# Batch 0's first score maxima from fp32 products instead of packed bf16 rows, with the splitting on GpSimd and values and batch 1's queries moved into the main loop

## The reference, cut to what matters

```python
x = x + tanh(g_xattn[0]) * attention(layernorm(x), ctx, ctx, Wq, Wk, Wv, Wo)
#   qh = einsum('bnd,hde->bhne', q, Wq);  kh, vh likewise from ctx with Wk, Wv
#   att = softmax(qh @ kh.T * 0.125);     out = concat_h(att @ vh) @ Wo.T
x = x + tanh(g_ffn[0]) * ffn(layernorm(x), router_w, w1, b1, w2, b2)
#   softmax over 8 experts, the top 2, gelu(x @ w1[e].T + b1[e]) @ w2[e].T + b2[e]
```

## Time and profile before

| | us |
|---|---|
| median of 3 runs | 1305.6 |
| lowest and highest run | 1301.69, 1305.78 |
| profiled execution, its own time | 1302.91 |
| its span, first to last instruction | 1301.1 |
| busy: TensorE | 1244.0 (96%) |
| busy: VectorE | 1130.9 (87%) |
| busy: ScalarE | 1083.0 (83%) |
| busy: GpSimd | 541.9 (42%) |

### The profile page before, as it was taken

One profiled execution on the slowest core, in us unless ns is written; L12 is line 12 of the kernel. 1 busy time (PEld: TensorE's weight loads), 2 busy tenths in 40 slices (PEclk: granted clock), 3 DMA queues, 4 the chain that ended last, 5 costly groups with the idle time before them and its releaser, 6 DMA issues.

```text
span 1301.1 us, 42169 instructions
## 1 busy us (share of the span) xinstructions
PE 1244.0 (96%) x16217; PEld 618.5 (48%) x16217; DVE 1130.9 (87%) x2076; ACT 1083.0 (83%) x2190; POOL 541.9 (42%) x1208
## 2 busy tenths in 40 slices
PE   4799999999999999999999999999999999999992
PEld 1243444444444444444444444444444444399982
DVE  7899999999999999999999999999999999355434
ACT  2588999989898999999999898999999898865661
POOL 3223435353626272626263534444353512146542
PEclk7799999999999999999999999999999999999996
DMA  3232221212121212131212122222211110288887
GB/s 95 83 87 74 59 82 52 75 48 79 48 78 47 80 46 84 39 92 31 76 48 74 55 68 62 63 67 60 69 56 44 50 41 7 77 267 242 259 267 244
DMA packets 61093, 112.94 MB, mean 87 GB/s; under 512 B 13053, under 2 KB 36477, under 8 KB 60749
## 3 DMA queue, kind: packets, MB, share of 16 engines
q1 hardware_dynamic: 54043, 97.67, 25.8%
q0 software_dynamic: 4320, 8.99, 2.0%
q10 hardware_dynamic: 2529, 3.58, 0.8%
HBM read 52.77 MB, written 13.71 MB: 51 GB/s over the span
## 4 chain that ended last, share of the span: by engine, by line
PE 83%; DVE 5%; POOL 4%; SPq 3%; issue 2%; DMA 2%; ACT 0%; POOLq 0%; DVEq 0%
PE pv L842 32%; PE st L784 18%; PE mxp L807 14%; PE st L764 7%; PE st L1058 5%; PE mxp L1068 5%; DVE mx L1568 3%; SPq L403 3%; POOL kf L632 1%; DVE x_sb L1766 1%; PE mxp L814 1%; POOL ksp L637 1%; PE st L920 1%; PE st L872 1%; POOL rows L695 1%
## 5 line engine op out<-in xcount | busy, mean ns | idle before, releaser
L1568 DVE TENSOR_REDUCE mx<-mxp 128x2 f32<-128x1024 f32 x768 | 914.3, 1216 | 38.5 <-PE mxp L807 33.4
L1097 ACT ACTIVATE arena<-st 128x512 f32<-128x512 f32 (+1 forms) x1664 | 884.5, 597 | 69.4 <-PE st L784 57.7
L842 PE MATMUL pv<-arena 128*32 128x256 f32 x6656 | 533.4, 392 | 0.5 <-ACT pv_sb L1104 0.3
L784 PE MATMUL st<-qpack,kpack 51*128 51x256 bf16 (+1 forms) x3328 | 483.7, 273 | 2.1 <-DMA qpack<-mxT 1.0
L807 PE MATMUL mxp<-kpack,qpack 48*128 48x512 bf16 x1536 | 414.8, 389 | 9.7 <-DVE mx L1568 9.4
L784 PEld LDWEIGHTS st<-qpack,kpack 51*128 51x128 bf16 (+1 forms) x3328 | 192.9, 96 | 276.3 <-ACT arena L1097 147.6
L842 PEld LDWEIGHTS pv<-arena 128*32 128x32 f32 x6656 | 131.4, 108 | 173.8 <-issue 107.7
L662 POOL CAST mxs<-nmx 128x8 bf16<-128x8 f32 x64 | 12.2, 191 | 391.5 <-DVE nmx L1579 391.4
L807 PEld LDWEIGHTS mxp<-kpack,qpack 48*128 48x128 bf16 x1536 | 120.6, 93 | 96.3 <-issue 46.8
L1238 ACT ACTIVATE arena<-st,bias 128x256 f32<-128x256 f32 (+1 forms) x172 | 74.9, 437 | 46.0 <-PE st L1058 42.1
L695 POOL DMA_INDIRECT rows<-xrow,pos x64 | 66.0, 1031 | 92.1 <-DVE pos L1423 77.0
(11 more groups left out here) (197 smaller groups left out, 953.7 us busy)
## 6 DMA issues: line engine op xcount, KB each, us to landing
kpack<-ksp SPq DMA_DIRECT2D x750, 50.0 KB
arena<-in_w12T SPq DMA_DIRECT2D x43, 576.0 KB
arena<-in_ctxT SPq DMA_DIRECT2D x15, 800.5 KB, 4.5
qpack<-qsp SPq DMA_DIRECT2D x187, 32.0 KB
xblk<-rows SPq DMA_DIRECT2D x28, 132.0 KB
rows<-in_pads SPq DMA_DIRECT2D x8, 264.0 KB, 4.7
arena<-results SPq DMA_DIRECT2D x8, 256.0 KB, 6.9
arena<-results ACTq DMA_DIRECT2D x8, 256.0 KB, 7.1
```

What stands on the lines that cost most here:

```text
L784: ins = eng.matmul(ring[i][0:n, jj * N:(jj + 1) * N], kpack[rows, b % 2, g * JJ + jj, kt * P:kt * P + n], qpack[rows, b % 2, g * JJ + jj, ...
L842: ins = eng.matmul(pv[32 * j:32 * j + 32, 0:N], vaug[0:n, b % 2, kt, at:at + 32], pt[0:n, (2 * u + rg) % PT_BUFS, jj * N:(jj + 1) * N], st ...
L1097: eng.activation(pt[0:n, c % PT_BUFS, :], ring[bank_of["S", u, p]][0:n, :], ACT.Exp, scale=SCALE).then_inc(s_exp, 1)
L1568: eng.tensor_reduce(mx[:, tj, w, :], src[:, :, 0:WIN], AX.X, ALU.max).then_inc(s_red, 1)
```

## The change

Batch 0's first 18 windows (`EARLY`) no longer read `kpack` and `qpack`. ScalarE copies the keys as fp32 to `kf`; the queries of each of four heads of a row group (`qearly`, in the room of the exponentials) are the fp32 queries times a column of zeros and ones (`head_rows`, made from the identity), two by VectorE (`early_queries`) and two by ScalarE (`later_queries`). A window is then one fp32 product over the 64 rows of the row group, masked down to one head (`early_window`). The splitting of batch 0's keys and queries goes from VectorE to GpSimd, whose rest is kept in `krest` and `qrest`; the layernorm of batch 0 goes from GpSimd to VectorE (`first_norm`). Memsets are shared out anew between VectorE and GpSimd. Three of the four value chunks, and x and queries of batch 1, go into units 1, 6, 7, 3 and 5 of the loop. Batch 1's keys are computed in units 8, 9, 10 and 17 in place of 6, 9, 10 and 11. Both row groups of group 2's keys are packed on SyncE's queue, after the first maxima are placed. Windows run one further ahead (`FIRST` 18, `LEAD` 23), and those of batch 0's loop (57 as before) stand at other units. The last reduction of a group is one instruction instead of two.

```diff
-FIRST_K_AT = {6: 0, 9: 1, 10: 2, 11: 3}
+FIRST_K_AT = {8: 0, 9: 1, 10: 2, 17: 3}
 RANK_AT, LAST_RANK_AT, COUNT_AT, PLAN_AT = 46, 35, 38, 40
 L_NORM_AT, X_NORM_AT = 10, 23
 LOGITS_AT, EXP_AT, ROUTE_AT = 24, 26, 26
 ROWS_AT, LAST_ROWS_AT = {1: 40, 2: 42, 3: 44}, {9: 0, 10: 1, 11: 2, 12: 3}
-FIRST, LEAD = 17, 22
+FIRST, LEAD = 18, 23
 WINDOWS_AT = ("0111111121010111101011111110111110110111101111111101",
               "0000100001000000010001000010000010010000100000000001")
-FIRST_WINDOWS_AT = ("0000110001001000000000000000101100000000010100100100",
-                    "1211110102111011111111112110101111112011101110011011")
+FIRST_WINDOWS_AT = ("0100201010210011010100000110111100010011000111211000",
+                    "1110002020001000010120201020001021011001110000000111")
 PER_BATCH = NG * NMX
+EARLY = FIRST
+EARLY_HEADS = -(-EARLY // NMX) * JJ
+FIRST_V, FIRST_TURN = 5, 14
+FIRST_V_AT, FIRST_X_AT, FIRST_Q_AT = {1: 1, 6: 2, 7: 3}, 3, 5
...
-    for c in range(NV):
-        take("V", 0, c)
+    take("V", 0, 0)
...
+        krest, qrest, qearly = carve(pt_f, [MP, N, EARLY_HEADS * N])
+        qearly = qearly.rearrange("p (h n) -> p h n", h=EARLY_HEADS)
...
-        k0p = [*st, mxp[0][:, 0, :]]
-        x_first, q_first = [mxp[0][:, 1, :], mxp[1][:, 1, :]], [mxp[1][:, 0, :], pv]
+        k0p, x_first, q_first = [*st, pv], mxp[1][:, 0, :], mxp[1][:, 1, :]
...
-            first_packs(eng, 0)
-            pack_query_rows(eng, 0, PARTS - 1, 1)
-            def other_keys(g):
-
-                for part in range(PARTS):
-                    pack_key_rows(eng, 0, g, part, 0)
-
-            other_keys(1)
+            first_keys_high(eng, 0)
+            first_query_rows(eng, range(PARTS), 0)
+            first_query_rows(eng, range(PARTS - 1, PARTS), 1)
+            first_keys_low(eng, 0)
+            other_keys(eng, 1, 0)
             eng.wait_ge(s_kone, 1)
             ones_rows(0)
-            other_keys(2)
             eng.wait_ge(s_mxT, 1)
             place_half(eng, 0, 0)
+            for rg in range(RG):
+                other_keys(eng, 2, rg)
             eng.dma_start(ctx_sb[:, 1, :], ctxT[1]).then_inc(s_ctx[1], 16)
             pack_keys(0, 3)
...
+            eng.memset(kone[:, :], 1.0).then_inc(s_kone, 1)
+            eng.memset(value_parts[:, 1, :, :, 0:VC], 0.0).then_inc(s_vone, 1)
+            eng.memset(vaug[:, :, :, VP * H:VW].rearrange("p k t w -> p (k t) w"), 0.0).then_inc(s_vone, 1)
+            split_keys(0, 0)
+            split_keys(0, 1)
+            split_queries(0)
+            split_keys(0, 2)
+            split_keys(0, 3)
             norm("X", 1)
+            split_maxima(0)
             split_queries(1)
-            split_maxima(0)
             for b in range(B):
...
+            def early_window(G, m, rg):
+
+                pair, rows = G * NMX + m, slice(rg * RSTEP, (rg + 1) * RSTEP)
+                if m == 0 and rg == 0:
+                    if G == 0:
+                        eng.wait_ge(s_qearly, JJ)
+                    else:
+                        eng.wait_ge(s_qlater, EARLY_HEADS - JJ)
+                if pair == 1 and rg == 0:
+                    eng.wait_ge(s_qhi, 1)
+                if pair < NF and rg == 0:
+                    eng.wait_ge(s_khi, pair + 2)
+                if pair >= MX_BUFS:
+                    eng.wait_ge(s_red, pair - MX_BUFS + 1)
+                if m < NMX - 1:
+                    tj, w = divmod(m, NF)
+                    t, jj = divmod(tj, JJ)
+                    ins = eng.matmul(mxp[pair % MX_BUFS][:, rg, 0:WIN],
+                                     qearly[rows, G * JJ + jj, t * P:(t + 1) * P],
+                                     kf[rows, w * WIN:(w + 1) * WIN], start=True, stop=True)
+                else:
+                    for tj in range(NT * JJ):
+                        t, jj = divmod(tj, JJ)
+                        ins = eng.matmul(mxp[pair % MX_BUFS][:, rg, tj * REST:(tj + 1) * REST],
+                                         qearly[rows, G * JJ + jj, t * P:(t + 1) * P],
+                                         kf[rows, NF * WIN:M], start=True, stop=True)
+                ins.then_inc(s_mxp, 1)
...
-                if m == 0:
+                if pair < EARLY:
+                    early_window(G, m, rg)
+                    return
+                if m == 0 or pair == EARLY:
                     eng.wait_ge(s_qd[b % 2], 16 * PACKS * (b // 2 + 1))
...
-            for c in range(NK):
+            for c in range(NK - 2):
                 keys(0, c)
             eng.wait_ge(s_id, 16)
             turn_rows("X", 0)
+            keys(0, NK - 2)
             eng.wait_ge(s_wq, 16)
             queries(0)
-            eng.wait_ge(s_wv, 16)
-            for c in range(NV - 1):
-                values(0, c)
-            turn_rows("X", 1)
-            queries(1)
+            keys(0, NK - 1)
             for n in range(issued(0, 0)):
-                if n == 1:
-                    eng.wait_ge(s_xnT, 2)
                 maximum(*divmod(n, NMX))
-                if n == 0:
-                    values(0, NV - 1)
-                elif n == NMX + 1:
+                if n == FIRST_V:
+                    eng.wait_ge(s_wv, 16)
+                    values(0, 0)
+                elif n == FIRST_TURN:
                     turn_maxima(0)
...
+                if b == 0 and r in FIRST_V_AT:
+                    values(0, FIRST_V_AT[r])
+                if u == FIRST_X_AT:
+                    turn_rows("X", 1)
+                elif u == FIRST_Q_AT:
+                    queries(1)
...
+            def first_high(c):
+                k0, kn = KCH[c]
+                eng.wait_ge(s_khi, c + 1)
+                eng.activation(ksp[:, 0, k0:k0 + kn], kf[:, k0:k0 + kn], ACT.Copy).then_inc(s_k0hi, 1)
+
+            def later_queries(h):
+                eng.wait_ge(s_heads, 1)
+                eng.wait_ge(s_qhi, 1)
+                eng.activation(qearly[:, h, :], qf[:, :], ACT.Copy, scale=head_rows[:, h:h + 1]
+                               ).then_inc(s_qlater, 1)
...
+            def early_queries():
 
                 nonlocal own
-                eng.wait_ge(*count)
-                eng.tensor_tensor(rest, src, three[0], ALU.subtract).then_inc(s_dve, 1)
-                eng.wait_ge(s_dve, own + 1)
-                eng.tensor_copy(three[1], rest).then_inc(s_dve, 1)
-                eng.wait_ge(s_dve, own + 2)
-                eng.tensor_tensor(three[2], rest, three[1], ALU.subtract).then_inc(done, 1)
-                own += 2
+                eng.wait_ge(s_id, 16)
+                eng.tensor_reduce(head_rows[:, :], id_sb[:, :].rearrange("p (x h) -> p h x", h=NP), AX.X,
+                                  ALU.add).then_inc(s_heads, 1)
+                eng.wait_ge(s_heads, 1)
+                eng.wait_ge(s_qp, 1)
+                for h in range(JJ):
+                    eng.tensor_scalar(qearly[:, h, :], q_first[:, 0:N], head_rows[:, h:h + 1], None,
+                                      ALU.mult).then_inc(s_qearly, 1)
...
+            eng.memset(value_parts[:, 0, :, :, 0:VC], 0.0).then_inc(s_vone, 1)
+            eng.memset(value_parts[:, :, :, :, VP - 1].rearrange("p k t h -> p (k t) h"), 1.0
+                       ).then_inc(s_vone, 1)
+            for ex in range(NE):
+                eng.memset(rank[:, ex:ex + 1], float(NE - ex)).then_inc(s_order, 1)
             for n in range(5):
                 norm_step("X", 0, n)
+            for n in range(4 * NEWTON + 1):
+                first_norm(n)
             eng.memset(taken[:, :], 0.0).then_inc(s_dve, 1)
             eng.memset(ge[:, :, NX:NX + 1], 0.0).then_inc(s_dve, 1)
             own += 2
-            vparts = vaug[:, :, :, 0:VP * H].rearrange("p k t (h c) -> p (k t) h c", c=VP)
-            eng.memset(vparts[:, :, :, VP - 1], 1.0).then_inc(s_vone, 1)
-            for c, (k0, kn) in enumerate(KCH):
-                split_first(k0p[c][:, 0:kn], kf[:, k0:k0 + kn],
-                            [ksp[:, n, k0:k0 + kn] for n in range(KINDS)], (s_khi, c + 1), s_k3)
-            split_first(q_first[0][:, 0:N], qf[:, :], [qsp[:, n, :] for n in range(KINDS)], (s_qhi, 1), s_q3)
             for n in range(5):
                 norm_step("X", 1, n)
-            eng.memset(kone[:, :], 1.0).then_inc(s_kone, 1)
-            for ex in range(NE):
-                eng.memset(rank[:, ex:ex + 1], float(NE - ex)).then_inc(s_order, 1)
-            eng.memset(vparts[:, :, :, 0:VC], 0.0).then_inc(s_vone, 1)
-            eng.memset(vaug[:, :, :, VP * H:VW].rearrange("p k t w -> p (k t) w"), 0.0).then_inc(s_vone, 1)
+            early_queries()
...
-            for c in range(NK):
-                first_keys(0, c)
+            first_keys(0, 0)
+            first_high(0)
+            first_keys(0, 1)
             copy_rows(0)
+            first_high(1)
+            first_keys(0, 2)
+            first_keys(0, 3)
             first_queries(0)
-            first_packs(eng, 1)
-            copy_rows(1)
-            for c in range(NV - 1):
```

(29 more changed lines are left out.)

130 lines of the change are left out of this document (82 added, 48 removed).

## The result

The changed kernel takes 1298.12 us, the median of six runs (1293.17 to 1301.64); the kernel before took 1304.92 beside it (1301.69 to 1307.42). The ratio is 0.9937, 95% interval 0.9914 to 0.996: faster, by more than the 0.3% that a measurement can tell. The profiled executions took 1296.63 and 1302.91 (spans 1294.8 and 1301.1). The kernels of the experiments were measured in three more sets, each beside the kernel before: between sets the ratios compare, not the times. This table sets the stretches of the two spans side by side, from the first scores of one batch to those of another.

A forecast was written before the change was run, and what follows sets the result against it. Bound: a chain of late packs and VectorE reductions before the loop, TensorE inside it. −6.8 + 1.5 − 0.3 = −5.6 us gave 1297.3, or 1300.0 on the median; it said 1299.0, range 1292 to 1305.

The forecast's parts named there:

- main term: Before the loop: first scores at 36.0 instead of 42.77 us, a gain of 6.8 us.
- Part 1: Before the loop: first windows wait only for fp32 keys and queries; first reduction at 11.8, 12 us earlier.
- Part 2: Early windows: an fp32 window costs 0.86 us of TensorE, its cycle is 1.14, all 18 end at 33.
- rival C: Before the loop: early windows become TensorE's, at 1.71 us or more each; no change or slower, up to 1334; chance 0.08.
- Part 3: Before the loop: splits end at 20.4, packs issue until 26.3, ones take 9.0 us; the loop starts at 36.0.
- rival B: Gain given back: GpSimd memsets delay splitting, moved work is paid in full, unit 8 stalls; 1302 to 1304, chance 0.19.
- Rival A: Ones drain quicker, windows set the loop's start at 33 to 34, clock stays up; 1292 to 1294, chance 0.16.
- Part 4: Batch 0's loop: of 2.7 us of TensorE work moved in, 1.5 us is paid; bounds 0 and 2.7.
- part 6: Batch 0's loop: group 2's and 3's packs, queued behind the placing, cost 0 at unit 8; bound 2 us of stall.
- Part 5: Loop: one window fewer is left for it, 0.27 us gained; one group reduction instead of two gains 0.
- Part 7: Loop's first units: clock may fall or stay up; taken as 0, or 6 us at half clock become 3.
- signs of a wrong premise: Batches 1 to 15: the premise is wrong if the loop's start and end differ from before by unlike amounts.

The follow-up runs named there:

- doubled products: The changed kernel with each 512-column product of the eighteen early windows issued twice: 1305.46 us, ratio 0.9982 to the kernel before.
- The experiment: The kernel with both edits, with value chunks 1 and 2 put back before the loop: 1294.95 us, ratio 0.9913 to the kernel before.
- both edits: The changed kernel with the ones issued first and group 2's packs before the first placing: 1293.49 us, ratio 0.99; on another chip 1294.38 us.

## Why the prediction was right, and where not

The time, 1299.0, lies 0.9 us from the median, and the main term held: 6.8 us earlier foretold, 6.49 measured. But several steps behind it failed, and their errors cancelled; that the time fits so closely is luck. The 1299.0 itself was chosen between the sum's 1297.3 and the 1300.0 that the medians make of it.

- **Part 1, first reduction at 11.8: it was 13.57.** The norm ended at 8.06 (8.1 forecast). What failed is the 2.6 us from there to the first product, which took 4.24: the third chunk of keys stands ahead of the queries in TensorE's order, and it ran for 1.56 us at half the clock, so that the projection ended at 11.21 and the masking began at 11.37. I had counted the norm's saving and left the front of the chain as it was. Part of the place is chance: the first reduction came at 12.76 to 14.81 in the nine kernels with early windows.
- **Part 2, price of a window 0.86: right,** by the doubled products. With it falls rival C, whose prices were 1.71 and more. **The cycle of 1.14: wrong, 1.24.** With two buffers it is half of the way from one product to the next in the same buffer: 1.20 us from the product's start to its reduction's (17.40 to 18.60) and 1.28 from there to the next product (16.12 to 17.40), where I had 1.14 for each. The delay behind a product was 0.26 to 0.28 where I took 0.18, and a reduction waited for took 1.22 where 1.14 is the pace of reductions in a row. So with the late first reduction the windows ended at 35.65 and not 33. The rule of the Trainium skill ("TensorE: Matmul & The Clock Gate", Part 3) that matmuls start and end in program order would have made a window 1.29 us; at 0.86 the trace disagrees with it again.
- **Part 3, packs and ones: right in the main.** Split end 20.54 (20.4), ones issued at 27.69 (26.3), scores at 36.28 (36.0): the packs took 1.4 us longer and the ones 1.0 less, which nearly cancels. The memsets ran at 0.9 ns a column and ended at 4.3, so rival B's first cause was none. The ones' 8.0 us stood for my 9.0. That they alone set the start was wrong: without them it came 0.4 us earlier, 0.8 counted from the first reduction. Rival A needed both, quick ones and windows that end at 33; it had neither.
- **Part 4, moved work, 1.5 us: mis-sized.** The experiment, one pair of traces, bounds it at 0.5 for 1.7 us of work. What batch 0 gave back came from part 6.
- **Part 5, one window fewer, −0.3: the step that failed most.** I priced the window's work and not its place. It is −3.0 in batch 15 and −0.6 to −1.2 in units 26 to 51: one window earlier, the last reduction is out of TensorE's way. I had read batches 1 to 15 as one row of 988.55 busy of 992.20; the stall stands in its last 2 us and is 1.55 of its 3.65 us of idle time.
- **Part 6, the packs, 0 with a bound of 2: wrong.** Against the kernel with both edits, units 8 and 9 lost 1.84 us. The packs landed at 52.1, 1 us behind the forecast's 51, but unit 8 began at 47.64 and not at 50 to 52, and ScalarE was ready for the copy at 49.55. Missing altogether was the placing for unit 26, 1.5 us, behind six packs: of a queue I had followed only the part up to unit 8.
- **Part 7, the clock, 0 (−3 if it stays up): it stayed up.** Units 0 to 7 gained 1.7 us. With 17 windows and the new table the half clock costs 2.2 there; with the old table less of it gave nothing. So clock and table seem to gain together.

In sum: start −6.5, batch 0 +1.0, last batch −3.0, the rest +2.2. Of the rest, the 0.9 of batches 1 to 14 are waits at unit 26 (2.3 us, 1.1 before); those batches took from 950.5 to 952.4 us in ten of the twelve traces. The end took from 169.4 to 172.6, and no cause was shown there. The lead alone gives 0.21% in the old kernel, and without it the change keeps 0.20% of its 0.63%: between a third and two thirds of the measured gain is the lead's, and a forecast of the right size came out of a sum that lacked it. One of the forecast's own signs of a wrong premise showed: at unit 52 the change is 5.45 us ahead of the kernel before, at the last scores 7.57, so the loop of batches 1 to 15 did not keep the start's gain as it was; it added the lead's.

## What to carry to other kernels

Where a stage loops many times at one engine's limit, look at its last turn by itself: a lead that costs nothing in the middle can decide whether the last wait there is idle time, and a short wait can pull the clock down after it. When a transfer leaves few partitions and carries many bytes, issue it where nothing waits behind it, and follow each queue it shares to the last consumer, not to the first. A transfer that lands just in time behind a long row of others has no slack: here every slow issue in front of it went through to TensorE. A term that moves the start of a saturated loop comes through for the most part (9.3 us of later start cost 6 to 10.6 here); the price of work moved into the loop depended on queue order more than on its own microseconds.

## What the runs showed of the hardware

- 150 KB of ones, read from 3 partitions in two issues, took 8.0 us from the first issue to landing (at 26 GB/s) and held up the issues of both queues behind them: six packs took 8.33 us. Issued first, ahead of every pack, they took 8.1 (7.14 to 15.23).
- A pack's issue took 0.61 us in the loop (0.65 from one to the next), and a few single ones took 1.6.
- The clock fell to half for short stretches behind idle time of TensorE: for 3.4 us behind gaps of 1.55 and 1.50 (at 1110.4 before, at 1108.6 with lead 22), for 6.8 around gaps of 2.79 and 4.56. The new wait for the packs can do it too: in the change's second profile TensorE stood for 1.55 us at 50.9 and the clock was at half from 54.2 for 3.4 us, while the first profile, with a wait of 1.63, kept 1.00. With the value chunks ahead, gaps of 0.76 and 0.52 near 38 stood before a stretch at 39.7; with both edits a gap of 0.76 at 36.4 was followed by none.
- A constant memset on GpSimd: 1872 fp32 columns in 1.76 us.
